# Written-out orders for four engines, separate tiles for the two norms, a last column in three pieces and filler matmuls at the start

## What is computed

```python
def _gn(v, G=32, eps=1e-05):                       # mean and variance per image and group of 2 channels
x = x + L0(_gn(x))
x = x + L1(_gn(x))

# L0: diffusion with gates
g  = relu(bn(dwconv(h, wg)));  g1 = relu(bn(dwconv(h, wg1)))   # two depthwise 3x3 convolutions
gy, gx = sobel(h)
Dx = 1/(gy*gy/4 + 1);  Dy = 1/(gx*gx/4 + 1);  D = 1/(1 + 2*Bx + 2*By)   # Bx = .2*Dx, By = .2*Dy
for _ in range(5):                                  # five steps, each needs the one before
    h = D*(c0*h0 - 2*E*h + cm_x*roll(h,1,2) + cp_x*roll(h,-1,2) + cm_y*roll(h,1,3) + cp_y*roll(h,-1,3))
    h = h + D*(2*DT)*fsrc;  h0 = prev
return relu(bn(h))

# L1: deformable 3x3 convolution
wi = conv(x, w_offset) + b_offset                   # 27 values a pixel: 9 row and 9 column offsets, 9 masks
sampled = bilinear(x at 9 moved places) * sigmoid(mask)
out = einsum('bkcp,fck->bfp', sampled, filt)
```

## Time and profile before

| | |
|---|---|
| median of 3 runs | 857.23 us (856.39 to 858.77) |
| profiled execution, its own time | 856.12 us |
| its span in the profile | 854.3 us |
| mean granted TensorE clock | 0.924 |
| busy in the span: TensorE | 740.4 us (87%) |
| VectorE, GpSimd, ScalarE | 527.2, 549.8, 203.8 us |
| DMA | 92.83 MB, of it 75.53 MB by the gathers |

### The profile page before, as it was taken

One profiled execution on the slowest core, in us unless ns is written; L12 is line 12 of the kernel. 1 busy time (PEld: TensorE's weight loads), 2 busy tenths in 40 slices (PEclk: granted clock), 3 DMA queues, 4 the chain that ended last, 5 costly groups with the idle time before them and its releaser, 6 DMA issues. The chain is left out here.

```text
span 854.3 us, 10727 instructions
## 1 busy us (share of the span) xinstructions
PE 740.4 (87%) x4130; PEld 551.5 (65%) x4130; DVE 527.2 (62%) x772; ACT 203.8 (24%) x401; POOL 549.8 (64%) x589
## 2 busy tenths in 40 slices
PE   5979979999999899989999999899999985764655
PEld 3545646677777677776777777677777664654544
DVE  5466558667775878657956795777767764422221
ACT  3302502151125212411333222411252001100000
POOL 1000037777777777777777777777777777777772
PEclk8999979999999999999999999999999998856565
DMA  6200033335333533353335333353335333533331
GB/s 192 67 16 1 15 81 107 106 106 159 113 107 102 163 113 106 103 163 107 110 107 154 115 113 105 114 153 111 105 106 162 111 105 106 162 112 106 107 111 46
DMA packets 53404, 92.83 MB, mean 109 GB/s; under 512 B 12313, under 2 KB 33641, under 8 KB 53353
## 3 DMA queue, kind: packets, MB, share of 16 engines
q0 software_dynamic: 27648, 75.53, 30.3%
q1 hardware_dynamic: 25704, 16.61, 7.2%
HBM read 79.70 MB, written 12.40 MB: 108 GB/s over the span
## 5 line engine op out<-in xcount | busy, mean ns | idle before, releaser
L392 POOL DMA_INDIRECT pixels<-table,index x576 | 546.7, 949 | 288.9 <-issue 175.2
L623 DVE TENSOR_TENSOR weighted<-pixels,banks 128x2304 f32<-128x2304 f32 x64 | 163.4, 2553 | 158.5 <-DMA pixels<-table,index 145.5
L799 PE MATMUL banks<-prod,const 128*128 128x448 f32 (+2 forms) x720 | 217.5, 441 | 15.9 <-DVE prod L543 15.9
L802 PE MATMUL banks<-const,weighted 128*128 128x128 f32 x1280 | 185.4, 298 | 44.4 <-DVE weighted L623 26.6
L802 PEld LDWEIGHTS banks<-const,weighted 128*128 128x128 f32 x1280 | 162.3, 157 | 70.8 <-ACT sampled_T L732 30.6
L799 PEld LDWEIGHTS banks<-prod,const 128*128 128x128 f32 x720 | 116.1, 195 | 90.9 <-issue 90.2
L732 ACT ACTIVATE sampled_T<-banks 128x512 f32<-128x512 f32 (+1 forms) x128 | 56.0, 437 | 334.7 <-PE banks L802 334.7
L543 DVE TENSOR_TENSOR prod<-coef,banks 128x1024 f32<-128x1024 f32 x80 | 95.5, 1215 | 51.7 <-PE banks L799 51.6
L799 PE MATMUL banks<-filt,sampled_T 128*128 128x64 f32 x640 | 89.2, 290 | 14.4 <-ACT sampled_T L732 7.9
L799 PEld LDWEIGHTS banks<-filt,sampled_T 128*128 128x128 f32 x640 | 83.1, 205 | 25.5 <-ACT sampled_T L732 17.2
L799 PE MATMUL banks<-conv_w,xT 128*128 128x384 f32 (+1 forms) x384 | 85.9, 380 | 0.0
(11 more groups left out here) (97 smaller groups left out, 477.5 us busy)
## 6 DMA issues: line engine op xcount, KB each, us to landing
pixels<-table,index POOLq DMA_INDIRECT x576, 2.8
table<-xn SPq DMA_DIRECT2D x48, 128.0 KB
table<-xn SPq DMA_DIRECT2D x16, 144.0 KB
x<-x_in SPq DMA_DIRECT2D x32, 64.0 KB, 2.1
out_dram<-x SPq DMA_DIRECT2D x64, 32.0 KB
table<-corner_w SPq DMA_DIRECT2D x16, 70.0 KB
const<-const_in SPq DMA_DIRECT2D x1, 768.0 KB, 5.6
table<-corner_w SPq DMA_DIRECT2D x8, 62.0 KB
```

The costliest lines, as they stand in the source:

```text
L392: pool.indirect_dma_start(out=pixels[:, col % NB, k, :], out_offset=None, in_=table[0:(u + 1) * TY * TX, :], in_offset=bass.IndirectOffset ...
L623: dve.tensor_tensor(weighted[:, col % 2, :, 0:K2, :].rearrange("p q k c -> p k q c"), pixels[:, col % NB, :, :].rearrange("p k (q c) -> p ...
L799: return pe.matmul(dst, lhsT, rhs, start=start, stop=stop, skip_group_check=True)
L802: return pe.matmul(dst, data, moved, start=start, stop=stop, is_transpose=True, skip_group_check=True)
```

## The change

The other parts, cut to their core:

```diff
-FIRST_FILLS = {"conv1": [("conv1", 4, "act", "gate1")]}
+FIRST_FILLS = {"turn": [("main1", 5, "act", "main1"), ("edges1", 6, "dve", "edges1")],
+               "conv1": [("conv1", 4, "act", "gate1")],
+               "own": [("own", 6, "dve", "coef0")]}
+WARM_UP = (8, 10, 9)
+LAST_TAPS = ((0, 6), (6, 8), (8, K2))
+            def warm_up(n):
+                for i in range(n):
+                    mm(banks[:, 6, 0:P], ones[:, :], ones[:, :], True, True)
                 if name == "sum1":
                     if n == 0:
-                        pe.wait_ge(s_const[0], 16)
+                        pe.wait_ge(s_ones, 1)
+                        warm_up(WARM_UP[0])
...
-                        mm(target(0), M["ones"], x1[0][:, :], True, True)
+                        mm(target(0), ones[:, :], x1[0][:, :], True, True)
+                        warm_up(WARM_UP[1])
...
+                    if (name, n) == ("sq1", 0):
+                        warm_up(WARM_UP[2])
```

```diff
-        xT = sb("xT", [P, 3, SLOTS * P])
-        gates = sb("gates", [P, WS, 2, C])
+        xT = sb("xT", [P, 2, 3, SLOTS * P])
+        gates = sb("gates", [P, 2, WC])
+        xc, squares = (p_arr, xc2), (r_arr, squares2)
+        gvar = [sb(f"gvar{i}", [P, GROUPS]) for i in (1, 2)]
...
+            def set_constants():
+                dve.memset(ones[:, :], 1.0 / (H * W * GROUP_SIZE)).then_inc(s_ones, 1)
+                dve.wait_ge(s_taps, 16)
+                dve.tensor_scalar(gate_bn[:, 3, :], gate_bn[:, 3, :], BN_EPS, None, ALU.add).then_inc(s_gate_ve, 1)
...
+            def depthwise(u, g, i):
+                dst = bank(u, f"conv{g}")
+                if i == 0:
+                    wait_bank_empty(u, f"conv{g}")
+                    mm(wc(dst), ones[:, :], every_col(shift_w[:, g, :], WS), True)
+                moved_rows(u, 1, i)
+                dh = ROW_ORDER[i]
+                ins = spread(dst, xT[:, 0, dh, :], conv_w[:, g, dh, :], SLOT_ORDER, C, WS, i == 2)
...
             def own_sums(u):
-                pe.wait_ge(s_gated, u + 1)
+                if u:
+                    pe.wait_ge(s_gated, 2 * u + 2)
+                    pe.wait_ge(s_force, u + 1)
+                pe.wait_ge(*emptied(u, "conv0"))
+                pe.wait_ge(*emptied(u, "conv1"))
```

```diff
-            load_x(0)
-            load_const(0)
+            for i in (0, 1):
+                load_side(sp, 0, i)
+            sp.dma_start(taps[:, :], taps_in).then_inc(s_taps, 16)
...
+            for i in (2, 3):
+                load_side(act, 0, i)
...
                 if u + 1 < UNITS:
-                    store(u, 0)
                     write_table(u + 1)
-                    store(u, 1)
...
+            sp.wait_ge(s_x2, UNITS * GROUPS_U + 1)
+            store_sides(sp, UNITS - 1, WS - 1, 1, (0, 1))
...
+            act.wait_ge(s_x2, UNITS * GROUPS_U + 1)
+            store_sides(act, UNITS - 1, WS - 1, 1, (2, 3))
...
+                for a, b in LAST_TAPS if col == LAST else ((0, K2),):
+                    if a == 0:
+                        dve.wait_ge(s_pixels[col % NB], (col // NB) * 16 * K2 + 16 * b)
+                    else:
+                        dve.wait_ge(arrived(col, a), 16 * (b - a))
+                    if b == K2 and col == LAST:
+                        add_columns(u, WS - COLS, COLS - 1)
...
+                    for i, taps_of in enumerate(LAST_TAPS[1:]):
+                        if col == LAST and taps_of[0] == 2 * k:
+                            pe.wait_ge(s_weighted, col + 2 + i)
```

More of the change, by code:

```diff
@@ L54 @@
[L54 to L81, removed]
@@ new lines @@
+copy1@54 copy0@55 copy1@55 copy0@56 copy1@56 copy0@57 copy1@57 copy0@58 copy1@58 copy0@59 copy1@59 copy0@60
+copy1@60 copy0@61 copy1@61 copy0@62 copy1@62 copy0@63 copy1@63"""
+PE_PIECES = """
+sum1+0 sq1+0 turn+0 gy+0 gx+0 conv0a+0 conv0b+0 conv0+0 conv1a+0 conv1b+0 conv1+0 init+0 edge+0 own+0 stx0+0
+sty0+0 sto0+0 sto1+0 stx1+0 sty1+0 sto2+0 stx2+0 sty2+0 sto3+0 sum1+1 stx3+0 sty3+0 sq1+1 sto4+0 stx4+0 sty4+0
+turn+1 shift+0 sum2+0 conv0a+1 sq2+0 gx+1 gy+1 conv0b+1 halo+0 turn2+0 conv0+1 off+0 conv1a+1 conv1b+1 conv1+1
@@ new lines @@
+init+1 edge+1 own+1 stx0+1 sty0+1 sto0+1 sto1+1 stx1+1 sty1+1 sto2+1 stx2+1 sty2+1 sto3+1 stx3+1 sty3+1 flip0@0
+flip1@0 flip0@1 filt@0 sto4+1 flip1@1 flip0@2 filt@1 stx4+1 sty4+1 sum1+2 shift+1 flip1@2 sq1+2 sum2+1 flip0@3
+filt@2 sq2+1 turn+2 flip1@3 gx+2 halo+1 conv0a+2 flip0@4 filt@3 turn2+1 gy+2 conv0b+2 off+1 conv0+2 flip1@4
+conv1a+2 flip0@5 filt@4 conv1b+2 conv1+2 flip1@5 init+2 flip0@6 filt@5 edge+2 own+2 stx0+2 sty0+2 flip1@6
+flip0@7 filt@6 sto0+2 flip1@7 sto1+2 stx1+2 sty1+2 flip0@8 filt@7 sto2+2 flip1@8 stx2+2 sty2+2 filt@8 sto3+2
@@ new lines @@
+stx3+2 sty3+2 flip0@9 sto4+2 flip1@9 sum1+3 flip0@10 filt@9 stx4+2 sty4+2 flip1@10 shift+2 sq1+3 sum2+2 flip0@11
+filt@10 sq2+2 turn+3 flip1@11 gx+3 halo+2 conv0a+3 flip0@12 filt@11 turn2+2 gy+3 conv0b+3 off+2 conv0+3 flip1@12
+conv1a+3 flip0@13 filt@12 conv1b+3 conv1+3 flip1@13 init+3 flip0@14 filt@13 edge+3 own+3 stx0+3 sty0+3 flip1@14
+flip0@15 filt@14 sto0+3 flip1@15 sto1+3 stx1+3 sty1+3 flip0@16 filt@15 sto2+3 flip1@16 stx2+3 sty2+3 filt@16
+sto3+3 stx3+3 sty3+3 flip0@17 sto4+3 flip1@17 sum1+4 flip0@18 filt@17 stx4+3 sty4+3 flip1@18 shift+3 sq1+4
@@ new lines @@
+sum2+3 flip0@19 filt@18 sq2+3 turn+4 flip1@19 gx+4 halo+3 conv0a+4 flip0@20 filt@19 turn2+3 gy+4 conv0b+4 off+3
+conv0+4 flip1@20 conv1a+4 flip0@21 filt@20 conv1b+4 conv1+4 flip1@21 init+4 flip0@22 filt@21 edge+4 own+4 stx0+4
+sty0+4 flip1@22 flip0@23 filt@22 sto0+4 flip1@23 sto1+4 stx1+4 sty1+4 flip0@24 filt@23 sto2+4 flip1@24 stx2+4
+sty2+4 filt@24 sto3+4 stx3+4 sty3+4 flip0@25 sto4+4 flip1@25 sum1+5 flip0@26 filt@25 stx4+4 sty4+4 flip1@26
+shift+4 sq1+5 sum2+4 flip0@27 filt@26 sq2+4 turn+5 flip1@27 gx+5 halo+4 conv0a+5 flip0@28 filt@27 turn2+4 gy+5
@@ new lines @@
+conv0b+5 off+4 conv0+5 flip1@28 conv1a+5 flip0@29 filt@28 conv1b+5 conv1+5 flip1@29 init+5 flip0@30 filt@29
+edge+5 own+5 stx0+5 sty0+5 flip1@30 flip0@31 filt@30 sto0+5 flip1@31 sto1+5 stx1+5 sty1+5 flip0@32 filt@31
+sto2+5 flip1@32 stx2+5 sty2+5 filt@32 sto3+5 stx3+5 sty3+5 flip0@33 sto4+5 flip1@33 sum1+6 flip0@34 filt@33
+stx4+5 sty4+5 flip1@34 shift+5 sq1+6 sum2+5 flip0@35 filt@34 sq2+5 turn+6 flip1@35 gx+6 halo+5 conv0a+6 flip0@36
+filt@35 turn2+5 gy+6 conv0b+6 off+5 conv0+6 flip1@36 conv1a+6 flip0@37 filt@36 conv1b+6 conv1+6 flip1@37 init+6
@@ new lines @@
+flip0@38 filt@37 edge+6 own+6 stx0+6 sty0+6 flip1@38 flip0@39 filt@38 sto0+6 flip1@39 sto1+6 stx1+6 sty1+6
+flip0@40 filt@39 sto2+6 flip1@40 stx2+6 sty2+6 filt@40 sto3+6 stx3+6 sty3+6 flip0@41 sto4+6 flip1@41 sum1+7
+flip0@42 filt@41 stx4+6 sty4+6 flip1@42 shift+6 sq1+7 sum2+6 flip0@43 filt@42 sq2+6 turn+7 flip1@43 gx+7 halo+6
+conv0a+7 flip0@44 filt@43 turn2+6 gy+7 conv0b+7 off+6 conv0+7 flip1@44 conv1a+7 flip0@45 filt@44 conv1b+7
+conv1+7 flip1@45 init+7 flip0@46 filt@45 edge+7 own+7 stx0+7 sty0+7 flip1@46 flip0@47 filt@46 sto0+7 flip1@47
@@ L327, in _ @@
             for u in range(1, UNITS):
[L328 removed]
+                for i in range(SIDES):
+                    load_side(sp, u, i)
             sp.wait_ge(s_zeros, 1)
```

527 lines of the change are left out of this document (327 added, 200 removed).

## The result

The changed kernel takes 827.73 us (median of 4 executions, 825.95 to 830.13) against 857.2: a ratio of 0.9656, with a 95% interval of 0.9628 to 0.9684. The profiled execution took 827.96 us for a span of 826.1. Run again beside other kernels, it took 829.04 (827.07 to 831.19) against 858.77. The forecast was 834 (826 to 845): the direction and the range held, and the gain is 29 us where 23 were worked out.

What follows compares the result with a forecast made beforehand. The prediction took GpSimd's closed row of 576 gathers as the bound. An earlier first gather (19.2 us) and a shorter tail (3.9) sum to 23.1 off 856.12, 833.0, plus 1.1 for the median: 834, range 826 to 845.

Steps and rivals of the forecast that it cites:

- The bound: GpSimd's 576 gathers, 1.254 us each, stay a closed row; only the first gather's start and the tail count.
- Until the norm: Start of image 0 up to its transposes: they start at 13.8 in place of 12.22, 1.6 us lost.
- The filler's start: Start of the kernel: filler begins once VectorE has set the ones, taken as 1.0 us, between 0.7 and 1.5.
- the second filler: Between image 0's two sums: the ten fillers stand on the path ahead of sq1 and cost 2.2 us.
- The clock: Image 0's transposes and Sobel filters: full clock throughout with filler, done at 20.4 where before it was 25.9.
- The convolutions to step 4: Image 0's gates and steps: 7.15 us a gate, step 4 ends at 71.4, 12.4 us earlier.
- From step 4 to the first gather: TensorE's own order sets the time: 23.7 us, then 3.2 to the gather, which starts at 98.3.
- the prologue: Everything before the first gather: it starts at 98.3 in place of 117.47, 19.2 us earlier.
- The middle: First to last gather: TensorE at 89.1 of 90.2 us an image, loss taken as 0 (range 0 to 6).
- rival 3: Middle: TensorE becomes the bound, indices come late at seven handovers; 871 us at 97 an image; chance 0.05.
- The tail: Behind the last gather: filt 2.8, smaller add 0.2, fewer stores 0.9, together 3.9 us saved; 5.5 at full clock.

Runs made afterwards that it cites:

- e6: The changed kernel with all of image 1's gate convolutions ahead of halo, turn2 and off of image 0: 838.3 us.
- e2: The changed kernel with four filler matmuls in place of ten between the two sums of image 0: 824.5 us.
- e1: The changed kernel with no filler matmuls at all at the start: 828.9 us.
- e9: The kernel of e2 plus 14 filler matmuls ahead of the transposes of each of the columns 59 to 62: 827.1 us.
- c0: The changed kernel run again without edits, as the yardstick: 829.0 us.
- e4: The changed kernel with gy and the rest of conv0 of image 1 moved behind image 0's offsets, ScalarE's and VectorE's pieces moved to suit: 827.5 us.
- e8: The changed kernel with three undoings for image 0: edges1 in bank 0, bnout ahead of cells and edges1, gx ahead of gy: 832.1 us (one execution).

## Why the prediction was right, and where its sum was short

**The bound.** Right: the gathers stayed a closed row of 1.254 us each, and e6 shows the first gather and the time moving one for one.

**Until the norm.** 1.6 us of loss worked out, 1.35 measured (13.57 against 12.22). The filler's start, an estimate of 1.0, was 1.05. That the total is so near is partly luck, since two sizes were off and cancel: `sum1` and the 512-column matmul, 2.2 in the sum, took 3.15, and a filler matmul took 0.47 and then 0.24 us, not 0.53 and 0.29. That the second filler stands on the path was right; six of its ten matmuls are worth 1.3 us (e2). Not foreseen: with the same filler T spreads from 12.0 to 13.6 between runs. The first ten records behind the filler took 1.92 in one execution and 3.15 in another; the full rate begins at another moment each time.

**The clock.** Full from the second filler on, as forecast; by the durations, the full rate begins within the ten records from 4.63 to 7.78. But I had credited the filler with both half-rate stretches of before (9.95 - 5.87 = 4.1 us); in the new order only one would come and cost 2.8 (e1), while T pays 0.6 to 2.2, so its net gain is 0.6 to 2.1 us of first gather. The Trainium skill says in "TensorE: Matmul & The Clock Gate", Part 1, that the gate is free-running and that a kernel varies by it from run to run. The variation is in the traces, at both ends of the kernel; that a free-running gate is its cause, no run here shows. Its Part 4 says that transposes don't count as busy in the same way. Nothing of that is visible here: the clock stayed at 1.00 across the transposes of image 0 (0.88 us), and 16 transposes in a row ran at full rate behind filler (1.97 us in e9).

The prediction counted two falls of the clock before; its traces show a third, in step 0. The 18 records took 6.86 us, against 5.19 after, behind an idle stretch of 2.74. From the kernel before, TensorE's step 0 and step 4 and a window:

```profile
48.48 6.86 PE L799 MATMUL banks<-prod,const 128*128 128x448 f32 x18 [2.74 <-DVE prod L543]
...
78.82 5.18 PE L799 MATMUL banks<-prod,const 128*128 128x448 f32 x18 [1.41 <-DVE prod L543]
```

```profile
50.00:52.00 2.00, 2.00 (x6) 1.18 (x6) 1.46 (x3) 0.00 (x0) 0.00 (x0) 0.50 0.05 17
```

Its sum holds this 1.7 us all the same, since it sets 5.2 at full clock against the 55.38 of before.

**The convolutions to step 4.** Forecast: step 4 done 57.6 behind T; measured 55.7. Each gate took 6.74 (26.62 - 19.88) where I had 7.15. The records of a gate are right (5.99 against 6.1); the step that failed is the adding up: I summed the durations of groups, and in the trace each group's end overlaps the next one's start by 0.1 to 0.2 us (19.88 + 1.08 is 20.96, the next starts at 20.80).

**From step 4 to the first gather.** Forecast 26.9, measured 25.65 (69.24 to 94.89), by the same slip over some dozen groups. With the 0.2 until the norm and the 1.9 until step 4 it is the 3.4 us that the prologue came out better than 19.2.

**What that gain is made of.** At the same points of the two timelines, image 0 is ahead of before by:

| point | before | after | ahead |
|---|---|---|---|
| transposes start (T) | 12.22 | 13.57 | -1.35 |
| gates start | 25.72 | 19.88 | 5.84 |
| step 0's matmuls start | 48.48 | 38.72 | 9.76 |
| step 0's matmuls end | 55.34 | 43.91 | 11.43 |
| step 4's matmuls end | 84.00 | 69.24 | 14.76 |
| offsets start | 110.09 | 87.51 | 22.58 |

So the Sobel filters give 7.2 us, the stretch to step 0 3.9, step 0 1.7, the steps 1 to 4 3.3 and the stretch to the offsets 7.8. By the undoings: image 1's second gate behind the offsets 9.0, the own product first 1.9, `edges1` early 1.85, the filler 0.6. These are 13.4 of 22.6, if they add, which no run tests. The rest (no wait of `own` for D times the gates, `turn`, `gx` and `own` of image 1 out of the way, and against them the dearer convolution) was not undone alone, and how it divides is open.

**The middle.** Nothing, as forecast: 0.8 us in this execution, 0 in c0. TensorE's load rose to 88.3 of 90.3 an image, and rival 3 did not come.

**The tail.** 3.9 us forecast with a half-rate tail; 6.5 in the profiled execution, because it ran at full rate. Over the nine profiles in which the changed tail is unaltered it takes 11.6 on average (8.7 to 13.7), close to the 12.0 that the sum gave. So the size was right for the usual case, and the tail of the profiled execution was a lucky one; its T was the latest of seven and its row 0.8 longer, so its total is near the median all the same. Taken over all profiles the miss is the prologue's: with the average T the first gather comes at 12.9 + 81.3 = 94.2, against 98.3.

## What to carry to other kernels

When one queue runs without gaps, split the span into what comes before its first element, the row itself and what comes after its last, and judge each edit by the stretch that it touches. A piece for the next image in front of a bounding piece of this one costs its length and the waits that come with it (e6: 9.0 us for 6.75); moved behind, it gives back its length less the waits that it had covered (e4: 4.25 of 5.4). It may go behind as long as the lead at the next handover lasts, and that lead has to be read for the image that follows. Filler pays only where it doesn't hold up what stands behind it (e1 against e2). Work out a chain on a pipelined engine from differences of start times, not from summed durations.

## What the runs showed of the hardware that I had not expected

The same instructions on TensorE ran at either rate in the tail, 1.92 or 3.68 us for 16 transposes, with idle gaps of up to 6 us ahead of them. The changed kernel's two tails, 9.5 and 13.6, differ by this alone as far as the profiles show. At the start the profile lists a granted clock of 1.00 while the matmuls run at half the later pace (16 records in 3.78 us, 20 later in 2.39), so for this stretch the durations tell the rate and the listed clock doesn't:

```profile
2.00:4.00 2.00, 2.00 (x12) 2.00 (x11) 0.34 (x1) 1.15 (x2) 2.00 (x1) 1.00 0.59 159
```

And a gap of 1.7 us from 15.7 did not bring the clock down (e8), while it fell within one of 2.7 us from 8.7 (e1), and within the last gap of 1.6 us in the tail of e9.
